# Half-tile score units and one-head masked maxima in a four-block attention kernel

## The chip, the cores and the metric

The kernel runs on one core of one Trainium2 chip. A time is the device time of one execution in microseconds. "Before" was run three times; its median is 3425.52 us (3421.22 to 3428.02).

The core's engines work side by side, each with its own queue: TensorE (PE), whose weight loads the profile shows apart (PEld), VectorE (DVE), ScalarE (ACT), GpSimd (POOL) and SyncE (SP), which starts the transfers. They meet at semaphores: each engine counts its finished work, and others wait for a count.

## The reference

Batch 4, sequence 512, width 256, a context of 1601 rows. Four blocks are applied one after the other, each gated and added to `x`:

```
x = x + tanh(g_xattn[0]) * xattn0(layernorm(x), ctx)            # block 1: 16 heads of 64, no mask
x = x + tanh(g_ffn[0])   * ffn0(layernorm(x))                   # block 2: 16 heads of 16 over 512, then a
                                                                #   top-2 mixture of 8 experts with capacity
x = x + tanh(g_xattn[1]) * xattn1(ctx, ctx, layernorm(x), mask) # block 3: 16 heads of 16 over 1601, masked
x = x + tanh(g_ffn[1])   * ffn1(layernorm(x))                   # block 4: 16 heads of 16 over 512 + 8 experts
```

All attentions are softmax attentions. Block 3 is the one that matters most here:

```
energy = einsum('nqhd,nkhd->nhqk', q, k)
energy = where(mask == 0, -1e20, energy)
attn = softmax(energy / sqrt(256), axis=3)
out = einsum('nhql,nlhd->nqhd', attn, v)
```

## The kernel before

**Slim attentions.** Blocks 2, 3 and 4 have heads of 16. Four heads make a group (`GROUPS` = 4 for each batch). A head's queries and keys lie in 32 partitions, so TensorE's array is used as 32x32 positions: a head stands on its own 32 rows of the array. A matmul of fp32 numbers shows as two records in the trace.

For each batch `b` and group `g` there are these units of work:
- `low`: queries for the maxima, in bf16.
- `max3` (block 3) or `maxb` (blocks 2 and 4): score products in bf16, of which only each query's maximum is kept. Block 3 has 32 `max3` for a group: 4 query tiles, 4 chunks of 401 context columns (`CTX_CHUNKS`), 2 pairs of heads. One unit is eight matmuls (two heads, four column groups) into one slot, and on VectorE two `tensor_tensor_reduce` of 401 columns which add the mask's row and take the maximum. Their thrown-away output goes to one of three places in turn (`max_junk`, in `rest` and `slim`).
- `negb`, `strip`, `rowb`: the maxima, negated and turned, are added to the fp32 queries. After `rowb` a group's scores may begin.
- `scoreb`: for 128 keys and all four heads, the score products in fp32. In block 3 a bf16 product of the mask comes first, into the same accumulation. A group has 13 such tiles in block 3 and 4 in blocks 2 and 4. ScalarE takes the exponential.
- `pvb`: the values times the exponentials of one tile, summed in the PSUM tile `pv`; it uses all rows of the array.
- `tailb`: the division by the sum, at a group's end. `outb` is the projection after four groups, `projqk`, `v4` and `expert4` are block 4's projections and expert products, which use the whole array.

**The ring.** PSUM holds `ring`, three slots of two banks, and `pv`. A unit that needs a slot waits until the engine that last read this slot has finished. A `max3` takes one slot, until VectorE has both its maxima. A `scoreb` takes two: heads 0 and 1 in the first, heads 2 and 3 in the second. Its matmuls for the first pair are sent after the first slot's wait; then PE waits for the second slot (`second_free`) and sends the rest. Nothing can stand between the two.

**The order.** `build_order` puts the units in one sequence, in which every engine takes its own part. Two streams of digits, `TURNS_1` up to the last `ranks` of block 2 and `TURNS_3` behind the experts, say which of eight generators gives the next unit (in `TURNS_3`: 1 block 3's scores, 2 its values, 3 its maxima, 5 to 7 block 4). `Pace` is a small planner which gives each unit a time on each engine. It decides which slot a unit takes (the one that it thinks free first) and where spare matmuls (`warm`) go in, which keep PE at work. It treats TensorE as one thing that is busy or not.

**The first group.** The first 32 `max3` of block 3 have no scores to go with. Three spare matmuls stand behind each.

## Time and profile before

| | us |
|---|---|
| median of three runs | 3425.52 |
| lowest, highest | 3421.22, 3428.02 |
| the profiled execution | 3398.36 |
| its span, first to last instruction | 3396.6 |
| PE busy in the span | 3242.2 |
| DVE, ACT, POOL busy | 1980.8, 1446.3, 955.0 |

The profile is of one execution. Its sections give the busy time of each engine, what released each wait, and the chain of work that ended last. The end of a matmul is modelled, and PE counts as busy when any part of its array is. "idle before" in brackets is time in which that engine did nothing ahead of the row; the arrow names the instruction that ended it. For PE the wait stands at the weight load (PEld), since the loads are sent first.

### The profile page before, as it was taken

Reading aid. Unit: us, or ns where it says so; the run is one execution under the profiler, and the core shown is the slowest. Engines: PE = TensorE matmul, PEld = TensorE weight load, DVE = VectorE, ACT = ScalarE, POOL = GpSimd, SP = SyncE. Lnnn points to the kernel's source line nnn. Section 1 sums busy time; section 2 is a strip of 40 time slices with the busy share of each in tenths; the row PEclk is TensorE's granted clock in tenths of the full one; section 3 lists DMA queues with packets and bytes.
Section 4 is the critical chain, followed back from the end, with each engine's and each line's share of the span. In section 5 each row is a group of like instructions: output and inputs, shape, how many; then the busy total and the mean of one; then the engine's idle time right before and its main releaser. Section 6 shows DMA issues by size and latency. Waiting matters only on the chain.

```text
span 3396.6 us, 71446 instructions
## 1 busy us (share of the span) xinstructions
PE 3242.2 (95%) x30986; PEld 1431.6 (42%) x31007; DVE 1980.8 (58%) x4289; ACT 1446.3 (43%) x1645; POOL 955.0 (28%) x469
## 2 busy tenths in 40 slices
PE   7999999999999999999997979899999999999999
PEld 3444444444434444444433753223333334343344
DVE  4444456554655546565575028677777777766446
ACT  3444344445434453344433212355454454545533
POOL 4655554654465445555400000100000000000000
PEclk9999999999999999999988999899999999999989
DMA  4000000000000000000021622565343444443300
GB/s 152 12 13 13 28 12 15 7 11 33 7 21 12 13 28 7 21 12 12 4 116 39 188 81 75 132 175 158 97 120 115 127 124 117 118 118 113 115 26 20
DMA packets 85306, 221.17 MB, mean 65 GB/s; under 512 B 18424, under 2 KB 39168, under 8 KB 84224
## 3 DMA queue, kind: packets, MB, share of 16 engines
q1 hardware_dynamic: 79616, 201.65, 19.5%
q0 software_dynamic: 5376, 14.95, 2.0%
q8 instruction: 244, 4.00, 0.5%
q14 instruction: 70, 0.57, 0.1%
HBM read 204.61 MB, written 18.48 MB: 66 GB/s over the span
## 4 chain that ended last, share of the span: by engine, by line
PE 84%; DVE 6%; ACT 4%; POOL 3%; issue 1%; DMA 1%; ACTq 0%; POOLq 0%; DVEq 0%
PE ring L1294 13%; PE pv L1179 10%; PE ring L1168 9%; PE pv L1310 9%; PE ring L1246 3%; PE ring L1149 3%; PE ring L1140 3%; PE ring L1126 3%; PE ring L1141 3%; PE ring L1165 3%; PE ring L1127 2%; PE ring L1290 2%; POOL wide L1554 2%; PE ring L1367 2%; PE ring L1348 2%; PE ring L1260 2%
## 5 line engine op out<-in xcount | busy, mean ns | idle before, releaser
L1554 POOL TENSOR_TENSOR wide<-wide 124x1024 f32<-124x1024 f32 (+1 forms) x341 | 803.9, 2358 | 180.2 <-ACT wide L1450 142.2
L1457 ACT ACTIVATE wide<-ring 128x1024 f32<-128x1024 f32 (+1 forms) x544 | 536.2, 1023 | 498.4 <-PE ring L1294 494.6
L1671 DVE TENSOR_REDUCE max_a<-ring 128x2 f32<-128x802 f32 x512 | 493.4, 991 | 395.9 <-PE ring L1149 395.5
L1450 ACT ACTIVATE wide<-ring 124x1024 f32<-124x1024 f32 (+1 forms) x416 | 425.3, 1026 | 438.1 <-PE ring L1168 385.0
L1294 PE MATMUL ring<-slim 32*32 32x512 f32 (+1 forms) x7040 | 522.9, 607 | 0.3 <-DVE slim L1724 0.2
L1699 DVE CUSTOM_DVE_ANT_0 rest<-ring,slim 128x401 bf16<-128x401 f32 x683 | 374.9, 576 | 106.0 <-PE ring L1246 71.1
L1168 PE MATMUL ring<-wide 64*124 64x512 f32 (+1 forms) x1664 | 424.7, 588 | 0.0
L1179 PE MATMUL pv<-wide 124*64 124x512 f32 (+1 forms) x1664 | 413.9, 613 | 8.2 <-ACT wide L1450 8.2
L1709 DVE TENSOR_REDUCE slim<-ring 128x2 f32<-128x1024 f32 x256 | 308.0, 1222 | 111.9 <-PE ring L1260 105.4
L1524 POOL DMA_DIRECT2D slim<-in_ctx_k x16 | 8.9, 558 | 968.5 <-PE ring L1246 920.2
L1551 POOL TENSOR_TENSOR wide<-wide 124x1024 f32<-124x1024 f32 x31 | 73.1, 2357 | 599.5 <-ACT wide L1450 586.2
L1699 DVE CUSTOM_DVE_ANT_0 slim<-ring,slim 128x401 bf16<-128x401 f32 x341 | 195.8, 574 | 59.1 <-PE ring L1246 46.8
L1310 PE MATMUL pv<-wide,slim 128*17 128x512 f32 (+1 forms) x1664 | 226.4, 617 | 0.0
L1294 PEld LDWEIGHTS ring<-slim 32*32 32x32 f32 (+2 forms) x7040 | 173.3, 110 | 114.6 <-issue 73.8
L1246 PE MATMUL ring<-slim 32*32 32x401 bf16 x4096 | 192.0, 347 | 21.4 <-ACT wide L1457 8.8
L1179 PEld LDWEIGHTS pv<-wide 124*64 124x64 f32 (+1 forms) x1664 | 99.0, 136 | 229.2 <-issue 201.4
L1168 PEld LDWEIGHTS ring<-wide 64*124 64x124 f32 (+1 forms) x1664 | 155.5, 183 | 73.0 <-issue 50.4
L1246 PEld LDWEIGHTS ring<-slim 32*32 32x32 bf16 x4096 | 59.8, 88 | 288.6 <-ACT wide L1457 152.1
L1165 PE MATMUL ring<-wide,select_b 64*128 64x512 bf16 x832 | 159.0, 379 | 8.1 <-ACT wide L1450 6.1
L1149 PE MATMUL ring<-wide 64*128 64x401 bf16 x1024 | 155.5, 337 | 9.7 <-DVE max_a L1671 4.7
L1290 PE MATMUL ring<-slim,ident_b 32*32 32x512 bf16 (+1 forms) x3264 | 154.0, 394 | 10.9 <-ACT wide L1457 8.2
L1140 PE MATMUL ring<-wide 128*124 128x128 f32 (+1 forms) x832 | 162.1, 276 | 0.4 <-DVE max_a L1671 0.4
(238 smaller groups left out, 3964.3 us busy)
## 6 DMA issues: line engine op xcount, KB each, us to landing
slim<-masks SPq DMA_DIRECT2D x832, 128.0 KB, 2.7
slim<-in_ctx_k SPq DMA_DIRECT2D x16, 800.5 KB, 4.6
wide<-in_w_pair SPq DMA_DIRECT2D x32, 384.0 KB, 3.0
wide<-in_w SPq DMA_DIRECT2D x16, 512.0 KB, 4.7
wide<-in_we SPq DMA_DIRECT2D x16, 512.0 KB, 3.7
slim<-in_ctx_v SPq DMA_DIRECT2D x16, 442.0 KB, 5.9
wide<-in_ctxT SPq DMA_DIRECT2D x4, 1601.0 KB, 6.8
slim<-in_ctx_k POOLq DMA_DIRECT2D x16, 400.2 KB, 4.8
```

Source lines behind the costliest of these rows:

```text
L1140: pe.matmul(place, ctxT[:, 0, k0:k0 + kn], pair_weights(p)[:, 2, 0, :], start=True, stop=False)
L1168: last = pe.matmul(slot[0:kn, h * BANK:(h + 1) * BANK], keys_a[own, p % 2, k0:k0 + kn], queries_a[own, p % 2, :], start=False, stop=True)
L1179: last = pe.matmul(pv_a[64 * h:64 * h + 64, :], values_a[0:kn, p % 2, k, 64 * h:64 * h + 64], exps_a[0:kn, slot_of["scorea", b, p, k], h * ...
L1246: last = pe.matmul(slot[j * PAD:(j + 1) * PAD, i * BANK:i * BANK + CHUNK], queries_low(3, g)[own, q * P + j * PAD:q * P + (j + 1) * PAD], ...
L1294: last = pe.matmul(head_bank(unit, h)[c0:c0 + cn, :], key_columns(blk, g, k0)[own, c0:c0 + cn], queries_place(blk, g)[own, :], start=blk ! ...
L1310: last = pe.matmul(pv_of[blk][PAD * h:PAD * h + rows_h, :], value_columns(blk, g, k, kn, h), exps_tile(blk, b, g, k, h)[0:kn, :], start=k ...
L1450: sc.activation(exps_a[0:kn, slot_of[unit], :], slot[0:kn, :], ACT.Exp, scale=WIDE ** -0.5).then_inc(scalar_done, 1)
L1457: sc.activation((exps_2 if blk == 2 else exps_34)[0:kn, first + 2 * i:first + 2 * i + 2, :].rearrange("p h n -> p (h n)"), ring_t[0:kn, ba ...
L1554: po.tensor_tensor(sums[0:kn, :], sums[0:kn, :], view, ALU.add).then_inc(pool_done, 1)
L1671: ve.reduce_max(max_a[:, :, q, c], slot.rearrange("p (h n) -> p h n", h=2)[:, :, 0:CHUNK], AX.X).then_inc(vector_done, 1)
L1699: ve.tensor_tensor_reduce(out=max_junk[junk], in0=slot[:, i * BANK:i * BANK + CHUNK], in1=maskQ_sb[:, q, CTX_CHUNKS[c]:CTX_CHUNKS[c] + CHUNK],
L1709: ve.tensor_reduce(neg_cols[blk][:, q, 2 * hp * PAD:2 * hp * PAD + PAD + 1:PAD], slot.rearrange("p (h n) -> p h n", h=2), AX.X, ALU.max, n ...
```

## The change

1. **Score tiles in halves.** A `scoreb` of blocks 2, 3 and 4 becomes two units, `("scoreb", blk, b, g, k, half)`. Each takes one slot, serves two heads, and has one exponential. They may stand apart in the order. In the order string each has its own digit.
2. **Masked maxima.** A `max3` unit is now one head and two chunks, where it was two heads and one chunk. It is still eight matmuls in one slot, but they use four positions of the array, each twice. VectorE takes both chunks with one `tensor_tensor_reduce` of 802 columns. For this `maskQ` is laid out by chunks of 401 (1604 columns), `max_b` gets two columns where it had four, the three `max_junk` places are twice as long, and some areas of `slim` move by four columns.
3. **The planner.** `Pace` has a busy time for each of the four row groups (`rows=`), and counts units on different rows as running side by side, each finished after its own time; `ISSUE` is the time between two sends. The two-slot parts go.
4. **The order.** `TURNS_1` is the old string with each 6 doubled. `TURNS_3` is new (1363 digits before, 1635 after).

```diff
-            turned = self.pe + (DIVIDE if step.parts[0] != self.parts else 0.0)
-            at = max(at, turned)
...
+            at = max(at, self.issued)
+            if step.parts[0] != self.parts:
+                free = max(self.busy) + DIVIDE
+            else:
+                free = max(self.busy[r] for r in step.rows)
...
+            self.issued = at + ISSUE
+            end = max(at, free) + step.pe
+            for r in range(4):
+                self.busy[r] = end if r in step.rows else max(self.busy[r], end - step.pe) if step.parts[0] != self.parts else self.busy[r]
+            self.pe, self.parts = max(self.busy), step.parts[1]
...
-    "maxb": (1, 0, 1, 0), "max3": (1, 0, 2, 0), "negb": (0, 0, 1, 0), "rowb": (1, 0, 1, 0),
-    "scoreb": (2, 2, 0, 0), "pvb": (1, 0, 0, 0), "tailb": (0, 1, 4, 0),
+    "maxb": (1, 0, 1, 0), "max3": (1, 0, 1, 0), "negb": (0, 0, 1, 0), "rowb": (1, 0, 1, 0),
+    "scoreb": (1, 1, 0, 0), "pvb": (1, 0, 0, 0), "tailb": (0, 1, 4, 0),
...
+            place = expo.take()
+            for half in range(2):
+                unit = ("scoreb", blk, b, g, k, half)
+                yield Step(lasts, (("sc", 1.02),), 1, (("rowb", blk, b, g),) + ((("pvb", blk, *behind),) if behind else ()), unit,
+                           divided, rows=(2 * half, 2 * half + 1))
+                plan.slot[unit], plan.slot_free[unit] = place, expo.free[place]
+                emit(in_slot(unit, "scalar"))
...
-                    b, g, q, hp, c = a
+                    b, g, q, h, c = a
...
+                    own = slice(PAD * h, PAD * (h + 1))
                     for i, j in product(range(2), range(P // PAD)):
-                        own = slice(PAD * (2 * hp + i), PAD * (2 * hp + i + 1))
+                        c0 = CTX_CHUNKS[2 * c + i]
...
-                    for first in (0, 2):
-                        if first:
-                            for lane, other in plan.second_free[unit]:
-                                past.wait_ge(*at(lane, *other))
...
+                    for i, (c0, cn) in product(range(2 if blk == 3 else 0), parts):
+                        own = slice(PAD * (2 * half + i), PAD * (2 * half + i) + cn)
+                        pe.matmul(slot[c0:c0 + cn, i * BANK:(i + 1) * BANK], ident_b[own, own],
+                                  mask_places[n % MASK_PLACES][own, c0 // PAD, :], start=True, stop=False)
...
+                    after(junk_free[0])
+                    ve.tensor_tensor_reduce(out=max_junk[junk].rearrange("p (i n) -> p i n", i=2),
+                                            in0=slot.rearrange("p (i n) -> p i n", i=2)[:, :, 0:CHUNK],
+                                            in1=maskQ_sb[:, q, 2 * c * CHUNK:2 * (c + 1) * CHUNK].rearrange("p (i n) -> p i n", i=2),
+                                            scale=1.0, scalar=-3e38, op0=ALU.add, op1=ALU.max,
+                                            accum_out=max_b[:, h, q, c:c + 1]).then_inc(vector_done, 1)
```

What this does to the order of instructions, at three places. In the fences a row is a line of the file, the operation, its tiles and the size of its output, and how often it follows itself. In before, L1246 is a masked maximum (eight matmuls), L1290 the mask and L1294 the scores of one pair of heads, L1310 a value step, L1260 a maximum of block 4.

PE before, block 3 in the first batch, one tile with four maxima between two value steps:

```order
L1310 MATMUL pv<-wide,slim 17x512 x4
L1246 MATMUL ring<-slim 32x401 x16
L1290 MATMUL ring<-slim,ident_b 32x512 x8
L1294 MATMUL ring<-slim 32x512 x8
L1290 MATMUL ring<-slim,ident_b 32x512 x8
L1294 MATMUL ring<-slim 32x512 x8
L1246 MATMUL ring<-slim 32x401 x16
L1310 MATMUL pv<-wide,slim 17x512 x4
```

PE of the changed kernel, the same batch; its L1244, L1283, L1287 and L1303 are the four of before:

```order
L1303 MATMUL pv<-wide,slim 17x512 x4
L1283 MATMUL ring<-slim,ident_b 32x512 x8
L1287 MATMUL ring<-slim 32x512 x8
L1244 MATMUL ring<-slim 32x401 x16
L1283 MATMUL ring<-slim,ident_b 32x512 x8
L1287 MATMUL ring<-slim 32x512 x8
L1244 MATMUL ring<-slim 32x401 x16
L1303 MATMUL pv<-wide,slim 17x512 x4
```

The two maxima that stood ahead of the tile now stand between its halves.

PE before, the last batch of block 4, behind a projection:

```order
L1294 MATMUL ring<-wide 32x512 x32
L1260 MATMUL ring<-wide 32x512 x8
L1310 MATMUL pv<-wide 17x512 x4
L1260 MATMUL ring<-wide 32x512 x8
L1294 MATMUL ring<-wide 32x512 x16
```

PE of the changed kernel there (L1287 scores, L1258 maximum, L1303 value step, L1098 spare matmuls):

```order
L1287 MATMUL ring<-wide 32x512 x16
L1098 MATMUL pv<-consts,ident_b 128x512 x2
L1258 MATMUL ring<-wide 32x512 x8
L1287 MATMUL ring<-wide 32x512 x8
L1258 MATMUL ring<-wide 32x512 x8
L1303 MATMUL pv<-wide 17x512 x4
```

The second tile's halves stand apart, with a maximum between them.

VectorE before and VectorE of the changed kernel, a group's masked maxima. First before:

```order
L1699 ISA rest,max_b<-ring,slim 128x401
L1699 ISA max_b 128x1
L1699 ISA slim,max_b<-ring,slim 128x401
L1699 ISA max_b 128x1
```

Then the changed kernel:

```order
L1688 ISA slim,max_b<-ring,slim 128x802
L1688 ISA max_b 128x1
```

One reduction of 802 columns stands for two of 401.

## Rows read from the trace of the kernel before

**Rows 1.** The page, summary: busy us (share of span) xinstructions.
```profile
span 3396.6 us, 71446 instructions
PE 3242.2 (95%) x30986; PEld 1431.6 (42%) x31007; DVE 1980.8 (58%) x4289; ACT 1446.3 (43%) x1645; POOL 955.0 (28%) x469
```

**Rows 2.** Stretches: length, busy PE PEld DVE ACT POOL, PEclk, DMA share, GB/s.
```profile
0.00:2010.80 2010.80, 1929.63 (x10499) 927.83 (x10507) 1030.31 (x1461) 821.32 (x972) 916.43 (x422) 0.98 0.11 35
2010.80:2078.60 67.80, 48.06 (x402) 17.92 (x411) 46.97 (x170) 2.43 (x5) 9.25 (x10) 0.87 0.10 28
2078.60:3264.70 1186.10, 1147.45 (x18911) 427.27 (x18912) 822.68 (x2527) 581.38 (x620) 29.37 (x37) 0.97 0.44 123
3264.70:3396.60 131.90, 117.06 (x1178) 58.62 (x1180) 80.88 (x131) 41.13 (x49) 0.00 (x0) 0.92 0.05 17
```

**Rows 3.** Waits of PE's loads, 2078.6 to 3264.7: us, times, longest.
```profile
PEld ring L1246 <- ACT wide L1457: 152.1, 196, 1.7
...
PEld ring L1290 <- DVE max_b L1699: 85.6, 147, 1.7
...
PEld ring L1246 <- DVE max_b L1699: 63.3, 97, 7.8
```

**Rows 4.** The costliest VectorE groups: shapes, count, busy us, mean ns, idle before.
```profile
L1671 DVE TENSOR_REDUCE max_a<-ring 128x2 f32<-128x802 f32 x512 | 493.4, 991 | 395.9 <-PE ring L1149 395.5
L1699 DVE CUSTOM_DVE_ANT_0 rest<-ring,slim 128x401 bf16<-128x401 f32 x683 | 374.9, 576 | 106.0 <-PE ring L1246 71.1 <-PE ring L1294 30.1 <-PE ring L1260 0.2
```

**Rows 5.** Timeline, two tiles of block 3: start us, length us, what, count.
```profile
2225.60 0.31 PEld L1246 LDWEIGHTS ring<-slim 32*32 32x32 bf16 x16 [0.85 <-ACT wide L1457]
...
2226.04 0.58 DVE L1699 CUSTOM_DVE_ANT_0 rest<-ring,slim 128x401 bf16<-128x401 f32 x1
2226.20 1.04 PE L1294 MATMUL ring<-slim 32*32 32x512 f32 x16
...
2226.54 0.57 DVE L1699 CUSTOM_DVE_ANT_0 slim<-ring,slim 128x401 bf16<-128x401 f32 x1
...
2227.17 0.11 PEld L1290 LDWEIGHTS ring<-slim,ident_b 32*32 32x32 bf16 x8 [0.84 <-DVE max_b L1699]
...
2227.40 1.04 PE L1294 MATMUL ring<-slim 32*32 32x512 f32 x16
...
2228.68 0.58 DVE L1699 CUSTOM_DVE_ANT_0 slim<-ring,slim 128x401 bf16<-128x401 f32 x1 [0.57 <-PE ring L1246]
...
2228.80 1.05 PE L1310 MATMUL pv<-wide,slim 128*17 128x512 f32 x8
...
2229.78 0.36 PE L1246 MATMUL ring<-slim 32*32 32x401 bf16 x8
...
2233.62 0.11 PEld L1246 LDWEIGHTS ring<-slim 32*32 32x32 bf16 x8 [0.85 <-ACT wide L1457]
```

**Rows 6.** Timeline, a masked maximum behind a second half.
```profile
2205.87 0.41 PE L1246 MATMUL ring<-slim 32*32 32x401 bf16 x8
...
2206.27 0.62 PE L1294 MATMUL ring<-slim 32*32 32x512 f32 x3
2207.02 0.58 DVE L1699 CUSTOM_DVE_ANT_0 slim<-ring,slim 128x401 bf16<-128x401 f32 x1 [1.77 <-PE ring L1294]
```

**Rows 7.** Timeline, two maxima behind a half, no value step.
```profile
2214.99 2.02 ACT L1457 ACTIVATE wide<-ring 128x1024 f32<-128x1024 f32 x2 [0.60 <-PE ring L1294]
...
2217.05 0.11 PEld L1290 LDWEIGHTS ring<-slim,ident_b 32*32 32x32 bf16 x8 [0.88 <-ACT wide L1457]
...
2218.45 1.02 ACT L1457 ACTIVATE wide<-ring 128x1024 f32<-128x1024 f32 x1 [1.45 <-PE ring L1294]
```

**Rows 8.** Timeline, both halves of a block 4 tile at once.
```profile
3245.79 1.16 PE L1294 MATMUL ring<-wide 32*32 32x512 f32 x32
```

**Rows 9.** Timeline, the first group's maxima, loads of two in a row.
```profile
2050.42 0.11 PEld L1246 LDWEIGHTS ring<-slim 32*32 32x32 bf16 x8 [0.42 <-DVE max_b L1699]
...
2051.46 0.11 PEld L1246 LDWEIGHTS ring<-slim 32*32 32x32 bf16 x8 [0.42 <-DVE max_b L1699]
```

197 lines of the change are left out of this document (83 added, 114 removed).

## The prediction

> I call a unit of slim scores a half-tile: eight 32x32 positions of the array (two heads, four column groups), one slot of the three-slot PSUM ring, one exponential. Two halves make a tile. A masked maximum (`max3`) also takes one slot. In the changed stretch there are 272 tiles (208 of block 3, 64 of block 4), 512 masked maxima and 128 maxima of block 4.
>
> **What bounds the kernel now.** First the page's summary, then the busy time by stage, then who ended each wait, then the timeline at single tiles. The summary shows PE busy for 3242 of 3397 us and no other engine over 58% [rows 1]. The stages [rows 2]: wide attention with block 2 and the experts fill 0 to 2011 us, the hand-over and the first group's maxima 68 us, the mixed stretch of blocks 3 and 4 1186 us, the last batch of block 4 132 us. In the mixed stretch PE counts as busy for 1147 us, but much of that is a part of the array working alone, and the weight loads show where the queue stood: before masked maxima and score tiles it waited 152 us for an exponential and 86 and 63 us for a maximum, each of which had to free a ring slot [rows 3]. So the stretch is bound by PE's own queue, which stops at slots, not by array work.
>
> The timeline shows one tile with four maxima [rows 5]. Two maxima load at 2225.60, the first half follows, and the second half's loads come only at 2227.17, after 0.84 us without a load, when a maximum has freed a slot. Its matmuls start 1.20 us after the first half's (2226.20 and 2227.40), although they stand on other rows of the array. Then two maxima and the value matmuls at 2228.80, and the next tile's maximum loads at 2229.78: 4.18 us. The next tile, with three maxima, begins there and ends at 2233.62: 3.84 us. Where two slots are free, both halves pass in 1.16 us together [rows 8], against 1.04 us of matmuls for one alone in [rows 5]; the stop between the halves costs about 1.1 us in this tile.
>
> **The change, part by part.** The first order string is the old one with each score digit doubled, and units and slots up to the experts stay where they were; the two-slot wait there stood between the halves already. I cost it, the experts and the differently laid out row mask (three columns more) at nothing: a stretch of 2011 us without a moved instruction. What the change can move is the 1386 us behind it.
>
> *Vector work.* Before, a masked maximum is two reductions of 401 columns, 576 ns each; a reduction over 802 columns takes 991 ns [rows 4], so 0.415 us for 401 columns more. In [rows 5] one reduction follows the other after 0.50 us (2226.04, 2226.54), so a unit holds the engine 1.00 us. The new unit needs 0.50 + 0.415 = 0.915 us. That is 512 x 0.08 = 43 us of vector work less. Only what PE waits for counts: about 290 waits for a maximum in the mixed stretch, the largest two groups being 147 and 97 [rows 3]. At 0.08 us each that is 23 us, at 0.15 us, where two follow each other, 43 us. In a tile with four maxima an exponential frees the next slot at nearly the same moment, so part is lost: I take -15 us, bounds -40 and 0.
>
> *Array work of a maximum.* Its eight matmuls now use four positions twice. In [rows 5] eight at once take 0.36 us; the second round adds 401 columns, about half of that, 0.17 us. Behind a score half this is hidden. It shows in some 50 of the 512, where a value step waits right behind: +8 us, bounds 0 and +30.
>
> *The halves apart.* Counted in the two PE orders, between one half and the next there stood nothing 289 times (272 of these within a tile), and now 144 times. New are two maxima alone (3 before, 41 now), two maxima and a value step (9, 88), one maximum alone (0, 66), a maximum and a value step (6, 51). What each costs depends on when the maxima behind a half are reported. In [rows 6] a maximum's matmuls start at 2205.87 and last 0.41 us, while the last three score matmuls, which stand ahead of them in the program, start at 2206.27 and last 0.62. Starts of separate rows of the array do pass each other. VectorE had been idle for 1.77 us when it began at 2207.02, after the scores' end at 2206.89: the maximum was reported after the half, not at its own end near 2206.28. The planner in the new file counts such a maximum as finished after its own 0.36 us, so it is reported some 0.6 us later than planned.
>
> The Trainium skill, "TensorE: Matmul & The Clock Gate", section "Why this matters for your kernels", says that concurrent matmuls complete in exact program order. By that rule the four-maximum tile below takes 4.9 us; by the planner's reading it would be 0.6 us shorter, since a maximum would free the next slot ahead of the exponential. The trace agrees with the rule on completion. The same page (section "Step-by-step: what each phase is for") has matmuls stay in program order altogether; for the starts [rows 6] differ, and the measurement decides.
>
> So the price of two maxima alone between halves is that of the three slots: half, maximum, maximum. The next half waits for the exponential. [rows 7]: exponentials end at 2217.01, the half loads at 2217.05, the next exponential starts at 2218.45; 0.04 + 1.40 + an exponential of 1.02 us is 2.46 us from half to half. A value step of 1.05 us fits inside. A four-maximum tile so written costs 4.92 us, against 4.18 before: 41 x 0.74 = **+30 us**, bounds +10 (if its neighbours make up for it) and +40.
>
> One maximum between halves: the second half needs the third slot, and ends about 1.1 us after the first, as it does now, but a maximum lies hidden in it. That maximum costs before what divides the two tiles of [rows 5], 4.18 - 3.84 = 0.34 us. Half of it is lost to the later report: 66 x 0.17 = **-11 us**, bounds -25 and 0.
>
> The 144 remaining neighbours: they now mostly follow a value step, so two slots have had a microsecond to come free, where before a maximum stood right ahead. The second half costs between 0.12 us [rows 8] and 1.2 us [rows 5], before mostly near the latter; I take a quarter microsecond less for half of them: **-18 us**, bounds -60 and 0.
>
> *The ends.* The first 32 maxima run alone, one in 1.04 us (2050.42 to 2051.46) [rows 9], with three spare matmuls behind each; 0.08 us less of VectorE, 0.17 us more of PE, which is about full there: between -3 and +5, taken +1. In the last batch three groups have maxima between the halves, each of 1.22 us on VectorE: 0 to +6, taken +3. No DMA moves by more than a unit: mask loads still follow the second half, and four places are ahead.
>
> **Sum**: -15 + 8 + 30 - 11 - 18 + 1 + 3 = -2 us. The profiled execution took 3398.4 us (span 3396.6), 27.1 us under the median of the runs shown, 3425.5. So 3396 us in a profile's terms, and **3423 us** in the median's. All low bounds together give -120 us, all high ones +80 us; they don't come together, so the case's own range is 25 us either way, 3398 to 3448.
>
> **The rivals.** *The plan holds* (faster): the halves are freed of the slot wait. Exponentials and maxima end 152 + 86 + 63 = 301 us of waits in [rows 3]. If 15% of these goes, 45 us, the time is 3380. For it speaks that the idle time ahead of second halves is real, and that expert steps now stand between halves in places, under which a slot comes free for nothing. Against it speak [rows 6].
>
> *The late report decides* (slower): 129 pairs of maxima stand right behind a half. If each pair's tile loses 0.74 us as in the sum above for those with a value step too, and only the neighbours' gain comes back, it is 129 x 0.74 / 2 - 18 = +30 us: 3455. VectorE then stands idle while a half ends and gets two maxima at once. [rows 5] already show that wait, 0.57 us before the first maximum behind a second half. The point from which it decides is about 70 such pairs.
>
> *The change does nothing*: if VectorE's shorter work and the order cancel because one chain (scores, exponential, slot) bounds both, the time is that of before, 3425; it lies inside the forecast's case. The granted clock is a price on top: 0.97 in the mixed stretch [rows 2]; a stop in a new place can cost or give 10 us, which widens the range.
>
> **How the numbers follow.** Gains and losses cancel to 25 us either way: 0.50. The plan holds: 0.26. The late report decides: 0.24. The least that a measurement can tell from no change is about 0.2%, 7 us. Inside the first case I split 0.18 faster, 0.16 same, 0.16 slower. Together faster 0.44, same 0.16, slower 0.40. The range takes in most of both rivals: 3365 to 3465.
>
> **What would show it.** The stretch up to the experts' end stays at 2011 us. A masked maximum is one reduction near 0.99 us, VectorE's busy time falls by about 40 us. Tiles written half, two maxima, half, two maxima, value step take 4.9 us (late report) or 4.3 (plan). The waits of [rows 3] for a maximum shrink, those for an exponential stay or grow. A maximum behind a half, with VectorE idle, starts after that half's end. I am wrong if the mixed stretch moves by over 25 us; then it shows in the length of those tiles, or in the waits of groups at rowb, which I left as they are.

## The result and the profile after

The changed kernel takes 3542.39 us (median of 4 runs, 3538.65 to 3544.89), the kernel before 3426.77 us (4 runs, 3421.22 to 3428.10): 1.034 of it, 95% interval 1.0322 to 1.0358. It is 116 us slower. The forecast was 3423 us, with a range that ended at 3465. The profiled execution took 3544.89 us; its span of 3543.1 us stands against 3396.6 us in [rows 1], 146.5 us more. That is more than the change costs, since the profiled execution of before was 27 us under its median. A second profile of the changed kernel (e8 below), beside a kernel before of 3399.64 us, has a span of 3503.7 us, 107 us over [rows 1]; amounts of time are therefore taken from e8. One execution of e13 below (4222 us, granted clock 0.73) was in a slower state and is left out of its median and ratio.

The page of the changed kernel, its summary (busy us, share of the span, instructions):

```profile
span 3543.1 us, 70384 instructions
PE 3336.2 (94%) x31007; PEld 1426.5 (40%) x31007; DVE 1941.8 (55%) x3265; ACT 1458.1 (41%) x1645; POOL 955.2 (27%) x469
```

VectorE has 39 us less to do than in [rows 1], as reckoned. PE shows 94 us more, although no product was added. The stretches of the changed kernel, columns as in [rows 2]:

```profile
0.00:2010.80 2010.80, 1930.23 (x10497) 925.55 (x10498) 1029.87 (x1460) 821.53 (x972) 916.54 (x422) 0.98 0.11 35
...
2010.80:2078.60 67.80, 49.44 (x354) 16.94 (x352) 40.05 (x95) 1.43 (x3) 7.71 (x8) 0.85 0.09 26
...
2078.60:3543.10 1464.50, 1356.48 (x20163) 484.06 (x20158) 871.83 (x1713) 635.13 (x670) 30.99 (x39) 0.91 0.36 101
```

Up to 2010.8 us nothing moved. All of the loss lies behind. The same last stretch of the kernel before, whose two parts stand in [rows 2], in one line:

```profile
2078.60:3396.60 1318.00, 1264.51 (x20086) 485.88 (x20090) 903.56 (x2658) 622.51 (x669) 29.37 (x37) 0.96 0.40 113
```

1464.5 against 1318.0 us: the whole 146.5. The granted clock is 0.91 where it was 0.96. In these two traces it has two levels, 1.0 and 0.5 (2.4 and 1.2 GHz), so a mean of 0.96 over 1318 us is about 105 us at the lower level, and 0.91 over 1464.5 us about 264 us. Added up record by record it is 101 and 256 us, and 192 us in e8.

The waits of PE's loads in the changed kernel, 2078.6 to 3419 us (us in total, times, longest), which answer [rows 3]. L1283 is the mask product with which a half begins, L1244 a masked maximum, L1303 a value step:

```profile
PEld ring L1283 <- DVE max_b L1688: 175.9, 148, 2.8
PEld pv L1303 <- issue: 157.6, 262, 1.7
PEld ring L1244 <- DVE max_b L1688: 94.7, 133, 2.4
...
PEld ring L1283 <- ACT wide L1448: 47.4, 55, 2.1
PEld ring L1244 <- ACT wide L1448: 38.3, 50, 2.4
```

A half waited 85.6 us for a maximum in [rows 3]; now it is 175.9 us (164.8 in e8), in the same number of waits (147 and 148): each is twice as long. A maximum waited mostly for an exponential (152.1 us), now mostly for another maximum. The waits of PE moved from ScalarE to VectorE, though VectorE has less to do.

The masked maxima among the costliest VectorE groups, to be held against [rows 4]:

```profile
L1688 DVE CUSTOM_DVE_ANT_0 slim<-ring,slim 128x802 bf16<-128x802 f32 x341 | 333.4, 992 | 193.2 <-PE ring L1287 113.4
...
L1688 DVE CUSTOM_DVE_ANT_0 rest<-ring,slim 128x802 bf16<-128x802 f32 x171 | 169.6, 992 | 90.0 <-PE ring L1287 61.6
```

992 ns, as estimated. And one turn of the new order's most frequent pattern (half, two maxima, value step) in the timeline of the changed kernel, at the full clock, as [rows 5] has the old one:

```profile
2584.37 1.05 PE L1303 MATMUL pv<-wide 128*17 128x512 f32 x8
...
2584.40 1.02 ACT L1448 ACTIVATE wide<-ring 128x1024 f32<-128x1024 f32 x1 [1.46 <-PE ring L1287]
2584.50 0.99 DVE L1688 CUSTOM_DVE_ANT_0 slim<-ring,slim 128x802 bf16<-128x802 f32 x1 [0.63 <-PE ring L1244]
...
2585.42 0.99 DVE L1688 CUSTOM_DVE_ANT_0 slim<-ring,slim 128x802 bf16<-128x802 f32 x1
2585.55 0.11 PEld L1283 LDWEIGHTS ring<-slim,ident_b 32*32 32x32 bf16 x8 [1.05 <-DVE max_b L1688]
...
2585.65 0.35 PE L1244 MATMUL ring<-slim 32*32 32x401 bf16 x4
...
2586.47 0.12 PEld L1244 LDWEIGHTS ring<-slim 32*32 32x32 bf16 x8 [0.56 <-DVE max_b L1688]
...
2586.92 1.05 PE L1303 MATMUL pv<-wide 128*17 128x512 f32 x8
2586.95 1.02 ACT L1448 ACTIVATE wide<-ring 128x1024 f32<-128x1024 f32 x1 [1.52 <-PE ring L1287]
```

From value step to value step 2.55 us, in which one half and two maxima pass. ScalarE works 1.02 us of it and waits 1.52 for PE, VectorE waits 0.63 for PE, PE waits 1.05 and 0.56 for VectorE. Nobody is full; the three pass three slots around. Two such turns are a tile with four maxima: 5.1 us.

### The profile page after: what moved, and what is told of

Same layout as the page of the kernel before. It is cut to its first block, busy times and chain, and to the rows that moved or that the text cites. A ratio compares the mean times of both kernels' runs of the same rounds, so it can differ in the third digit from the quotient of the medians.

```text
span 3543.1 us, 70384 instructions
## 1 busy us (share of the span) xinstructions
PE 3336.2 (94%) x31007; PEld 1426.5 (40%) x31007; DVE 1941.8 (55%) x3265; ACT 1458.1 (41%) x1645; POOL 955.2 (27%) x469
## 4 chain that ended last, share of the span: by engine, by line
PE 82%; DVE 7%; issue 4%; ACT 3%; POOL 3%; DMA 1%; DVEq 0%; SPq 0%; POOLq 0%; ACTq 0%
PE ring L1287 14%; PE pv L1176 10%; PE ring L1165 9%; PE pv L1303 8%; PE ring L1283 3%; PE ring L1244 3%; PE ring L1146 3%; PE ring L1137 3%; PE ring L1123 3%; PE ring L1138 3%; PE ring L1162 2%; PE ring L1124 2%; POOL wide L1544 2%; PE ring L1360 2%; PE ring L1341 2%
## 5 line engine op out<-in xcount | busy, mean ns | idle before, releaser
L1448 ACT ACTIVATE wide<-ring 128x1024 f32<-128x1024 f32 (+1 forms) x544 | 548.4, 1024 | 617.5 <-PE ring L1287 569.0
L1287 PE MATMUL ring<-slim 32*32 32x512 f32 (+1 forms) x7040 | 579.2, 642 | 1.5 <-issue 1.0
L1688 DVE CUSTOM_DVE_ANT_0 slim<-ring,slim 128x802 bf16<-128x802 f32 x341 | 333.4, 992 | 193.2 <-PE ring L1287 113.4
L1244 PE MATMUL ring<-slim 32*32 32x401 bf16 x4096 | 266.8, 363 | 10.9 <-DVE max_b L1688 3.9
L1303 PE MATMUL pv<-wide,slim 128*17 128x512 f32 (+1 forms) x1664 | 260.3, 689 | 3.8 <-ACT wide L1448 3.4
L1283 PE MATMUL ring<-slim,ident_b 32*32 32x512 bf16 (+1 forms) x3264 | 169.9, 413 | 62.6 <-DVE max_b L1688 46.8
L1688 DVE CUSTOM_DVE_ANT_0 rest<-ring,slim 128x802 bf16<-128x802 f32 x171 | 169.6, 992 | 90.0 <-PE ring L1287 61.6
L1287 PEld LDWEIGHTS ring<-slim 32*32 32x32 f32 (+1 forms) x7040 | 171.0, 114 | 115.9 <-issue 80.6
L1283 PEld LDWEIGHTS ring<-slim,ident_b 32*32 32x32 bf16 (+1 forms) x3264 | 48.7, 88 | 299.3 <-DVE max_b L1688 175.9
```

The lines of the kernel that those rows point to most:

```text
L1244: last = pe.matmul(slot[j * PAD:(j + 1) * PAD, i * BANK:i * BANK + CHUNK], queries_low(3, g)[own, q * P + j * PAD:q * P + (j + 1) * PAD], ...
L1283: pe.matmul(slot[c0:c0 + cn, i * BANK:(i + 1) * BANK], ident_b[own, own], mask_places[n % MASK_PLACES][own, c0 // PAD, :], start=True, sto ...
L1287: last = pe.matmul(slot[c0:c0 + cn, i * BANK:(i + 1) * BANK], key_columns(blk, g, k0)[own, c0:c0 + cn], queries_place(blk, g)[own, :], sta ...
L1303: last = pe.matmul(pv_of[blk][PAD * h:PAD * h + rows_h, :], value_columns(blk, g, k, kn, h), exps_tile(blk, b, g, k, h)[0:kn, :], start=k ...
L1448: sc.activation((exps_2 if blk == 2 else exps_34)[0:kn, first:first + 2, :].rearrange("p h n -> p (h n)"), slot[0:kn, :], ACT.Exp, scale=D ...
L1688: ve.tensor_tensor_reduce(out=max_junk[junk].rearrange("p (i n) -> p i n", i=2), in0=slot.rearrange("p (i n) -> p i n", i=2)[:, :, 0:CHUNK ...
```

## The experiments

Eighteen kernels were run, in five groups, each group beside the kernel before on one chip. That one took 3398.5 to 3428.3 us in them, so ratios to it are compared, not times. "Low clock" is the time at the lower level behind 2078.6 us, added up from the clock records of the one profiled execution. Last lines of stretches are shown once, here, in the columns of [rows 2]; all run from 2078.6 us to the kernel's end. In this order: e8 (the changed kernel again), e1, e3, e4, e7, e9, e15, e16:

```profile
2078.60:3503.70 1425.10, 1318.15 (x20149) 479.52 (x20155) 871.36 (x1711) 634.74 (x670) 30.93 (x39) 0.93 0.37 104
```
```profile
2078.60:3430.20 1351.60, 1302.14 (x20118) 500.69 (x20122) 870.67 (x1705) 623.02 (x670) 30.72 (x39) 0.96 0.39 110
```
```profile
2078.60:3506.10 1427.50, 1324.70 (x20090) 481.11 (x20095) 903.49 (x2658) 634.01 (x670) 30.31 (x38) 0.93 0.36 104
```
```profile
2078.60:3467.00 1388.40, 1270.10 (x20095) 470.71 (x20100) 866.49 (x1701) 634.53 (x670) 30.94 (x39) 0.95 0.38 107
```
```profile
2078.60:3390.90 1312.30, 1259.55 (x20093) 485.73 (x20096) 866.01 (x1699) 622.84 (x670) 30.32 (x38) 0.96 0.41 113
```
```profile
2078.60:3493.90 1415.30, 1320.41 (x20084) 473.43 (x20089) 905.16 (x2657) 629.32 (x668) 28.38 (x36) 0.93 0.37 105
```
```profile
2078.60:3520.80 1442.20, 1359.09 (x20116) 495.59 (x20121) 912.14 (x2671) 630.76 (x670) 30.80 (x39) 0.92 0.36 103
```
```profile
2078.60:3585.10 1506.50, 1377.74 (x20120) 495.72 (x20124) 897.69 (x2673) 624.96 (x670) 30.71 (x39) 0.90 0.34 99
```

The results in one table; the texts follow below.

| kernel | order of the last half | maxima | ratio to before | 95% interval | low clock, us |
|---|---|---|---|---|---|
| before | old | old | 1 | | 101 |
| e7 | old | one reduction, two strips | 0.9945 | 0.9925 to 0.9964 | 98 |
| e1 | old | new | 1.0126 | 1.0089 to 1.0163 | 119 |
| e4 | new | one reduction, two strips | 1.0212 | 1.0180 to 1.0245 | 133 |
| e6 | new, slots in turn | new | 1.0293 | 1.0268 to 1.0318 | 209 |
| e8 (after) | new | new | 1.0320 | 1.0288 to 1.0352 | 192 |
| e3 | new | old | 1.0335 | 1.0288 to 1.0382 | 211 |
| e10 | new | new, each issued twice | 1.0527 | 1.0495 to 1.0560 | 182 |

### Order or maxima: e1, e3, e8

The first theory: the new order costs the time. The rival: the maxima do, which now stand on one strip of the array.

e1, the last half's order of before in the changed kernel (first line of the table; 1 and 5 are the score streams of blocks 3 and 4, 3 the stream with the masked maxima, 2 and 6 the value steps):

```diff
 TURNS_3 = (
-    "00333333333333333333333333333333333333333131113213313321331332313133213313321331332133133231323133113233331132"
+    "00333333333333333333333333333333333333333331133311332311303231133233201111323323111120113233231133323113332331"
...
```

> The changed kernel with the last half's order of before (the old table, with a digit that stood for a score tile written twice, since a tile is now two steps). The maxima are the new ones: one head, two chunks, one reduction. If the new order is what costs the 116 us, this is near before, 3415 to 3440 us. If the one-head maxima cost it (344 in the slim part, on one row strip each, 0.36 us of one position where it was 0.17), it stays near after, above 3480 us. If both do a share, it lies between.

e3, the old maxima in the changed kernel:

```diff
-                for c in range(len(CTX_CHUNKS) // 2):
-                    for h in range(GROUP):
+                for c in range(len(CTX_CHUNKS)):
+                    for hp in range(2):
...
+                    for i in range(2):
+                        after(junk_free[0])
+                        ve.tensor_tensor_reduce(out=max_junk[junk][:, 0:CHUNK], in0=slot[:, i * BANK:i * BANK + CHUNK],
+                                                in1=maskQ_sb[:, q, c * CHUNK:(c + 1) * CHUNK],
...
```

> The changed kernel, its order and its planner, with the maxima of before: two heads and one chunk, two reductions of 401 columns. If the new order costs the time, this is as slow as after or slower, 3530 to 3580 us, since VectorE has 0.13 us more for each maximum. If the one-head form of the maxima costs it, this is near before, 3420 to 3450 us.

> The changed kernel, unchanged, beside the others on one chip: ratio to before 1.032 to 1.036, as recorded. It is the yardstick for the kernels of this call.

Measured: 1.0126, 1.0335, 1.0320. (Some expectations count 344 masked maxima. The file has 512, of which 32 belong to the first group.) The order alone, with the old maxima, costs all of it (e3). With the new maxima it costs 1.9% (e8 against e1). But the new maxima alone, in the old order, cost 1.3% (e1), where a gain of 15 us was reckoned. Both theories are half right, and the parts don't add up: 3.35 and 1.26 would be 4.6, the two together give 3.2.

### One strip and one reduction: e4, e7

The new maximum differs in two things: one reduction instead of two, and eight matmuls on four positions instead of eight. e4 takes them apart:

```diff
-                    own = slice(PAD * h, PAD * (h + 1))
                     for i, j in product(range(2), range(P // PAD)):
+                        own = slice(PAD * (h ^ i), PAD * (h ^ i) + PAD)
                         c0 = CTX_CHUNKS[2 * c + i]
```

> The changed kernel, where each maximum's second chunk is taken with the neighbouring head's rows (its maxima are mixed over two heads, so the shifts are others): eight matmuls on eight positions, as before, instead of two rounds on four, and everything else unchanged. If what costs is that a one-head maximum runs its two chunks one after the other on one strip, the time falls by up to 344 x 0.19 = 65 us, to 3475 to 3500 us. If the order or the slots cost it, it stays within 10 us of 3542.

> The changed kernel with the order of before (as the first experiment) and, as in the fourth one, each maximum's second chunk taken with the neighbouring head's rows, so that eight matmuls stand on eight positions (the maxima are mixed over two heads; the shifts are others). Against the first experiment (ratio 1.013 to before) only the array positions change, against before only the single reduction. If one strip costs the same in any order, about 1.3%, this is at or under before: ratio 0.995 to 1.002. If one strip costs only through the slots of the new order, it stays at 1.010 to 1.015.

Measured 1.0212 and 0.9945. So the one strip costs 1.8% in the old order (e1 against e7, some 61 us) and 1.1% in the new one (e8 against e4, 37 us). The single reduction gives 0.55% in the old order (e7 against before, 19 us) and 1.2% in the new one (e4 against e3). The new order costs 2.7% (e4 against e7) with everything else alike. Two cautions: e7 also has the new file's planner and slots, and e3's planner picks other slots than that of e4, so the single reduction isn't quite alone in either pair.

Where the strip is felt shows in the value steps' waits, which need all rows of the array. The waits of value steps' loads, 2078.6 to 3419 us, in e1 and in e7:

```profile
PEld pv L1303 <- issue: 112.4, 273, 0.8
```
```profile
PEld pv L1303 <- issue: 96.0, 273, 1.6
```

A value step behind a one-strip maximum waits 0.34 us in the timelines, behind a two-strip one 0.18 (e4). The two lines differ by 16 us. PE's busy time tells more: 1302.1 us in e1, 1259.6 in e7. The rest is spread thinly: from the end of one score half to the end of the next, with three maxima and a value step between them, it is 2.87 us in e1 and 2.77 in e7 (68 times, means at full clock). That it is the products on the maximum's own rows which wait is argued, not shown. In the new order the low clock differs more, 192 us in e8 and 133 in e4.

### Slots in turn: e6

```diff
-        self.picked = sorted(range(RING), key=lambda i: self.ring[i])[:step.slots]
+        if self.turned:
+            self.picked = [self.turn % RING][:step.slots]
+            self.turn += len(self.picked)
```

> The changed kernel in its own order, but in the last half the three score slots are taken strictly in turn. The new planner, which reckons maxima as done beside the half in front of them, gives 235 units of the last half the slot of the unit two before them (79 in the kernel before), although the matmuls are seen to complete in order. If waiting for such slots costs the time, this is 30 to 80 us faster than after, 3460 to 3510 us. If the order itself costs it, it stays within 10 us of 3542.

Measured 1.0293, on the same chip as e1, e3 and e4; e8 has 1.0320. At most 0.3%, and the intervals overlap. The planner's choice of slots isn't what costs.

### The halves apart: e9, e11, e12, e13, e14

e9 leaves the old order and the old maxima, and moves one step of the maxima's stream between the halves wherever one stood right behind them (113 becomes 131):

```diff
-    "00333333333333333333333333333333333333333331133311332311303231133233201111323323111120113233231133323113332331"
+    "00333333333333333333333333333333333333333331313313132313103231313233201113123323111120131233231313323131332331"
...
```

> The old order and the old maxima (two heads, two reductions), with one edit: in 152 places of the last half a step of the maxima's stream that stood behind the second half of a tile now stands between its halves; in 135 of them it is a maximum. In the trace of before two halves side by side are reported 0.50 us apart in the mean; with one maximum between them they are 1.8 us apart in the changed kernel. If it is the parting of the halves that costs, it is about 135 x 0.4 = 54 us, ratio 1.010 to 1.025. If only two maxima in a row behind a half cost (the price of the forecast), one between is free or a gain: 0.990 to 1.003.

Measured 1.0295: 97 us for 135 maxima, 0.72 us each. The forecast had the opposite sign for it (-0.17 us each). From the end of a first half to the end of its second half, by the records of their last matmuls, it is 0.89 us in the mean in the kernel before (272 tiles), 1.31 us in e9 (1.83 for its 135 parted ones) and 2.64 us in the changed kernel (e8). The 0.50 us in the expectation is too low. The blocks differ: in block 3 of the kernel before it is 1.10 us in the mean and 1.08 in the median (208 tiles), in block 4 0.23 and 0.10 (64 tiles).

The 1.08 us of block 3 is no wait for a slot. In 76 of the 208 tiles the second half's mask products start within 0.5 us of the first's, so both slots were free, and the halves still end 1.08 us apart. The kernel before has such a tile at 2249.56 us; this one is the changed kernel's, behind a value step and at full clock:

```profile
2315.74 0.52 PE L1283 MATMUL ring<-slim,ident_b 32*32 32x512 bf16 x16
...
2315.96 2.12 PE L1287 MATMUL ring<-slim 32*32 32x512 f32 x32
```

The score products of both halves take 2.12 us together, twice the 1.04 of one, while the same 32 records take 1.16 us in block 4 ([rows 8]). Why block 3's halves don't overlap is open. So 1.08 us is there with or without a wait, and a maximum between the halves comes on top of most of it: 1.70 us at full clock for the parted tiles of e9 (105 of them) against 1.05. The timeline of e9:

```profile
2545.76 0.41 PE L1282 MATMUL ring<-slim,ident_b 32*32 32x512 bf16 x8
...
2546.41 0.12 PEld L1243 LDWEIGHTS ring<-slim 32*32 32x32 bf16 x8 [0.30 <-DVE max_b L1688]
...
2547.30 0.11 PEld L1282 LDWEIGHTS ring<-slim,ident_b 32*32 32x32 bf16 x8 [0.77 <-DVE max_b L1688]
```

The second half's mask products start 1.54 us behind the first's, and waited for the slot of a maximum. A third of the 97 us is clock (below): e9 has 191 us of low clock.

The reverse, then: the changed kernel with every pair of halves side by side again, what stood between them behind (e11) or half ahead and half behind (e12); e13 and e14 are the same orders with the old maxima. The first line of e11:

```diff
-    "00333333333333333333333333333333333333333131113213313321331332313133213313321331332133133231323133113233331132"
+    "00333333333333333333333333333333333333333113113211333321133332311333211333321133332113333231132333113233331132"
...
```

> The changed kernel with its own order, but the two halves of every tile are put side by side again: in 174 tiles of the last half what stood between them (maxima, value steps, experts) now stands behind the second half. Everything else keeps its place, and the maxima are the new ones. If the parting of the halves is what the new order costs (0.72 us for each of 135 in the experiment before), most of the difference to the old order goes: ratio to before 1.010 to 1.020, where after is 1.032 and the old order with these maxima 1.013. If the rest of the order (which tile gets which maxima, experts and value steps) costs it, the ratio stays over 1.025. The runs of maxima are longer than in either order (four and a value step 16 times), which may cost some of it.

> As the one before, but half of what stood between the halves is put ahead of the first half and half behind the second, so that maxima are spread more evenly. Ratio to before 1.005 to 1.020 if the parting costs; over 1.025 if not.

> The order of the kernel with the halves side by side and the rest behind, with the maxima of before (two heads, two reductions). If parting and the one-strip maxima together hold the whole loss, this is near before: ratio 0.995 to 1.010. If the order costs otherwise, it stays over 1.015.

> The order with the halves side by side and the rest spread on both sides, with the maxima of before. Ratio 0.990 to 1.010 if parting and one-strip maxima hold the whole loss; over 1.015 otherwise.

Measured 1.0352, 1.0577, 1.0263 and 1.0534 (intervals of 0.2 points either way), low clock in e11 155 us, in e12 342. All four came out where the expectations put them if the rest of the order costs it, and far from the gain that parting alone would have meant. Parting the halves of the old order costs 3%; joining those of the new one gives back 0.7 points with the old maxima (e13 against e3) and nothing with the new ones (e11 against e8). What a parted tile costs depends on where its maxima would stand otherwise.

The traces have a price for that, much the same in both kernels of the table. The time from the end of a half to the end of the next, by what stands between them (block 4's maxima counted in; number of places, and mean at full clock in us):

| between two halves | before | changed (e8) |
|---|---|---|
| nothing | 289: 0.85 | 144: 0.92 |
| one maximum | none | 66: 1.37 |
| a value step | 11: 2.10 | 24: 2.16 |
| one maximum, a value step | 10: 2.27 | 57: 2.17 |
| two maxima | 3: 2.32 | 41: 2.53 |
| two maxima, a value step | 55: 2.59 | 111: 2.54 |
| three maxima, a value step | 68: 2.81 | 22: 2.66 |

A value step beside two maxima costs nothing more in e8, and a third maximum 0.1 to 0.2 us. In e16 below, four maxima and a value step take 3.60 us (82 places). What costs is to open such a place at all. Before has 254 places with something in them, the changed kernel 399. An estimate from the mean prices of all the kernels at full clock puts the new order 50 to 60 us above the old one. The same sum gives 40 us at most for e15 and e17, so it doesn't explain these two.

### How many maxima in a tile: e15 to e18

In the kernel before, tiles with one value step and 0, 1, 2 or 3 maxima (block 4's counted in) last 2.7, 3.8, 3.2 and 4.1 us, from one second half to the next; those with four and two value steps 5.6. (The expectation of e15 has 3.5 us for the first and 5.9 for the last.) Of its 272 tiles, 73 have two and 94 three. The new order has 74 tiles with four and 56 with none: it puts a group's maxima early, four to a tile, and leaves bare tiles at the end. So the third theory was: the price bends upwards, and the new order pays for being uneven. e16 crams the old order in this way, e15 makes it more even; e17 and e18 make the new order even.

```diff
-    "00333333333333333333333333333333333333333331133311332311303231133233201111323323111120113233231133323113332331"
+    "00333333333333333333333333333333333333333113333113323311330233113323320113333113323321133331133233011221121121"
...
```

> The maxima and the order of before, halves side by side, with each group's maxima put as early as they go, four to a tile, and none in the group's last tiles, as the new order has them: tiles with 0, 1, 2, 3 and 4 maxima are 87, 32, 17, 6 and 129. By the prices of before this costs some 110 us: ratio 1.025 to 1.040, like after, with none of the halves parted and none of the maxima changed. If unevenness is not what costs, it stays under 1.010.

> The maxima and the order of before, halves side by side, with the maxima of each group spread more evenly over its tiles: tiles with 0, 1, 2, 3, 4 and over 4 maxima are 32, 18, 93, 116, 12 and 1, where before has 50, 18, 73, 94, 29 and 8. Price of a tile by its maxima, in the trace of before: 0: 2.3 us, 3.5 with a value step; 1: 3.7; 2: 3.4; 3: 4.15; 4: 5.9; 5: 6.7. By these prices it saves some 40 us: ratio to before 0.985 to 0.995. If the number of maxima in a tile does not matter, only their sum, it stays within 0.3% of before, or is slower for whatever else the moves upset.

> The changed kernel's own order and maxima with the halves side by side, as in the eleventh kernel (ratio 1.035), and the maxima of each group spread evenly: tiles with 0, 1, 2, 3 and 4 or more maxima are 28, 28, 86, 117 and 13. If unevenness is what the order costs, this comes down to what the one-strip maxima cost in the old order: 1.005 to 1.018. If not, it stays over 1.025.

> The changed kernel's own order and maxima, with the value steps, experts and fourth block's steps that part halves left where they are (99 tiles stay parted), and only the masked maxima spread evenly, none of them between halves in block 3: tiles with 0, 1, 2, 3 and 4 or more maxima are 32, 15, 110, 94 and 21. If unevenness costs the most and a value step between halves little, 1.010 to 1.025; if parting costs by itself whatever stands between, over 1.025.

Measured: e16 1.0472, e15 1.0263, e17 1.0396, e18 1.0809. Cramming costs what was expected and more, with no half parted and no maximum changed. But the even orders lose as well, and e18, where value steps part 99 tiles, is the slowest of all. So the number in a tile is not the law either. In e15 one piece can be named. About from the first group's row step to the second's, e15 and then the kernel before:

```profile
2082.80:2171.90 89.10, 76.83 (x929) 19.31 (x929) 43.95 (x157) 28.52 (x29) 7.21 (x8) 0.59 0.32 88
```
```profile
2079.50:2137.60 58.10, 52.46 (x935) 16.25 (x939) 43.07 (x157) 27.12 (x28) 6.54 (x8) 0.88 0.51 134
```

The same units (929 and 935 matmuls recorded) in 89.1 us at a clock of 0.59, and in 58.1 us at 0.88. A third of e15's loss of 93 us is this one group.

### Maxima beside experts: e19, e20

e15 had also moved maxima away from expert steps, which keep PE for 3.5 us and need neither ScalarE nor, until their end, VectorE. e20 does this alone for 16 maxima, e19 moves 13 the other way.

```diff
-    "23113233421155323411336411424371132331133231143231136355323311323336437355243341137113446355324113635532337113"
+    "23113233421155323411336411424711332331133231143231136355323311323336437355243341137113446355324113635532711333"
...
```

> The maxima and the order of before, halves side by side, with 13 masked maxima moved ahead, from behind the next tile to right behind an expert step (3.5 us of matmuls for which ScalarE has nothing to do, so a slot and VectorE are free there). If a maximum beside an expert step is free and one in a tile costs some 0.75 us, this is 5 to 10 us faster than before: ratio 0.997 to 0.9985. If its place makes no difference, within 0.1% of before.

> The reverse: 16 masked maxima that stand beside an expert step in before moved behind the next tile. If the cover of the expert steps is what the evened order gave away (it had moved maxima out of there too), this is 12 to 20 us slower than before: ratio 1.0035 to 1.006. If the evened order lost by something else, it stays within 0.15% of before.

Measured: e20 1.0047 (1.0033 to 1.0062), as expected; e19 1.0032 (1.0015 to 1.0049), a miss: it was to be faster. Both moves cost. A caution: e9 and e13 to e16, e19 and e20 use the new file's planner. With the old order and the old maxima it lets 20 of the last half's 1328 slot uses follow on another unit than in the kernel before. That combination was not run, so an offset of a few tenths of a per cent common to e19 and e20 can't be excluded. Against the 2.6 to 4.7% of the others it doesn't matter.

### The clock: e10, and a reading of all traces

> The changed kernel, where each masked maximum's eight matmuls are issued twice (the same values to the same place), 16 in all, so the array is busier between slots and a maximum 0.35 us longer. In the changed kernel the clock stands at its lower level for 256 us of the last half (101 before), with PE 68% busy in the 4 us ahead of most of these spells. If the low clock costs much, the added work keeps it up and pays for a part of itself: at most 20 us slower or even faster than after, and under 150 us of low clock. If the length of the maxima is what costs, it is 50 to 150 us slower than after (344 x 0.35 = 120 us).

```diff
-                    for i, j in product(range(2), range(P // PAD)):
+                    for _, i, j in product(range(2), range(2), range(P // PAD)):
```

Measured 1.0527, 71 us over e8, low clock 182 us against 192. More array work did little for the clock, and it cost a good part of its own length (512 x 0.35 = 179 us at most). What brings the clock down is not settled. Just ahead of its falls PE is shown busy 69% of the time in the changed kernel (median of 44 spells), 68% in the kernel before (14 spells), but 88% in e10 (25 spells).

What a spell costs can be read, since kernels with one order have it in different groups. The last half was cut at the 16 row steps of block 3 and the two last projections. For before, e1 and e7, and for e3, e4, e6 and e8, the length of each piece was set against its low-clock time, with a mean of its own for every piece and every kernel. The slope is 0.37 +- 0.04 us and 0.39 +- 0.03 us for each us of low clock (standard errors). The repeated executions of one kernel on one chip say the same: over 148 executions of 23 such sets, the time grows by 0.39 +- 0.01 us for each us of low clock, the latter reckoned from each execution's mean clock and span. By this, the 91 us more of low clock in e8 are some 35 of its 107 us, e9's 90 us are 35 of its 97, and of the 37 us between e8 and e4 the clock makes 23. Set beside the kernel before on its own chip, e15 has 97 us more of low clock and e18 353: 38 of 93 us and 138 of 276. The rest of these losses isn't clock.

## Why the prediction was wrong, point by point

What failed above all is the price of the order (the part "The halves apart"): forecast at +1 us, it is 91 us. The single terms:

**The first 2011 us unchanged**: right. PE is busy for 1930.2 us there, against 1929.6 in [rows 2].

**Vector work, -15 us (-40 to 0)**: right. The reduction takes 992 ns, VectorE's busy time fell by 39 us, and the single reduction gives 15 to 19 us in the old order (e7; by the slope above some 8 of it come with the clock), 40 in the new.

**Array work of a maximum, +8 us (0 to +30)**: right in kind, mis-sized. It is 61 us in the old order (e1 against e7) and 37 in the new. The step that failed is "behind a score half this is hidden": the value steps wait longer, places with maxima take 0.1 us more, and in the new order there are 59 us more of low clock.

**Two maxima between halves, 41 x 0.74 = +30 us**: the turn was right, the count was not. A turn takes 2.55 us (2.46 forecast), and with a value step in it it is the same: in e8, at full clock, two maxima between halves take 2.53 us in the mean (28 times) and two maxima and a value step 2.54 (72 times). The text itself said that "a value step of 1.05 us fits inside", and then priced only the 41 pairs without one. All 129 at 0.74 us are 95 us. The 0.74 rests on one tile of 4.18 us; against the four maxima together of e16 (3.60 + 1.08 = 4.68 us) two turns cost 0.4 us more, and 129 of them some 50 us. The rival "the late report decides" had them, but halved the sum without a row to show for it, and came to +30.

**One maximum between halves, 66 x -0.17 = -11 us**: wrong sign. e9 has +0.72 us each, about 0.5 without the clock. The base was right: the second half ends about 1.1 us after the first in block 3. The step that failed is that it "ends about 1.1 us after the first, as it does now, but a maximum lies hidden in it". With a maximum between them the halves are 1.70 us apart in e9 at full clock. In the changed kernel such a place takes 1.37 us, 0.5 more than one with nothing in it (0.85); and a maximum taken out of a place with three saves about 0.2 us, not 0.34.

**The remaining neighbours, -18 us (-60 to 0)**: there is no sign of it. In block 3 at full clock they end 1.07 us apart in e8 (93 places) and 1.04 in the kernel before (212). The failed step is the lower bound, 0.12 us by [rows 8]: that row is of block 4. In block 3 the second half ends 1.08 us after the first even with both slots free, so two free slots give nothing back, and the "stop between the halves" of [rows 5] was mostly no stop.

**The clock, 10 us either way**: mis-sized, about 35 us (e8).

**Completion in order**: nothing here speaks against it. The late report of [rows 6] is seen again in the turn shown above (VectorE idle 0.63 us before the first of two maxima). So the new planner reckons short. By its own sums the last half takes 1272 us in the new order and 1344 in the old; made to complete in order it has 1323 for the new one. Of the 72 us that it saw to gain, 51 vanish so. It still prefers the order that the chip runs slower, so this is not its only error: it has no clock, and it runs block 3's halves side by side.

The planner also says something on the experiments that could have been known ahead. By its sums the last half takes 1405 us in e9, 1377, 1412, 1404 and 1452 in e13 to e16, and 1374, 1400, 1402 and 1433 in e11, e12, e17 and e18, against 1344 in the old order. It has the sign right for every order that was moved by hand, but reckons the loss 30 to 190 us smaller than it is against before. Only the order that comes with the change, which it rates best, does it rate wrongly. So the slowness of the moved orders is weak evidence on why the new one is slow.

In sum: of the 3.2% of e8, the order makes 2.7, the one strip 1.1, and the single reduction gives 0.55 back (they are e7, e4 and e8 in turn: -0.55, +2.67, +1.08; taken in another turn the order is 1.9 or 3.35, so these are shares along one path). The order's 30 - 11 - 18 = +1 us stand against 91 us (2.67%). Two gains that don't exist, -11 and -18, cancelled a loss that was counted for a third of its places; that the strip's 8 us were 37 comes on top. The chance of 0.40 for "slower" was spread over sums that ended at +40 us.

What stays open: which property of an order decides. Parting halves (e9), cramming (e16), evening (e15, e17, e18) and joining (e11 to e14) of the two orders all lose against before, by 2.6 to 8%, and low clock goes along (e18: 471 us, e16: 310). The prices of places explain about half of the new order's loss and the clock about a third; why evened orders have more low clock, and what the rest of their loss is, none of the three theories says.

A version that beats both with each head's own maxima was not found. e7 is faster than before by 0.55%, but it mixes two heads' maxima; the same layout with the right values needs a second copy of the low queries and keys in the neighbouring strips, with a product or a copy more for each of 16 groups. That wasn't tried.

## What to carry to other kernels

Price a changed order by the mean of a kind of gap over the whole trace, not by one tile, and price every gap of the same kind; and take the row for a bound from the same block, since two halves pass in 1.16 us in block 4 and in 2.12 in block 3. A planner that orders work on concurrent rows must report in program order, or it sees a gain that isn't there (51 of 72 us here). And a unit made cheaper on one engine (one reduction instead of two) isn't cheaper if it stands twice as long on the array that all wait for: swap one part at a time. Here only the single reduction paid, in e7.

## What the runs showed of the hardware

- Two halves on separate rows of the array, side by side in the queue, end 0.10 us apart in block 4 (median of 64) and 1.08 us apart in block 3 (median of 208), there also when both slots are free; with a maximum between them 1.72 us (median of 135, e9).
- The clock falls without a long stop. In the changed kernel PE's loads wait 2.8 us at most for a slot of a maximum in the mixed stretch, and it still has 256 us of low clock, in 44 spells.
- A us at the lower clock costs 0.37 to 0.39 us here; but one group can stay there for most of its length (89.1 us at a clock of 0.59 in e15).
- An order with the same work can be 6.7% slower (e18 against e1, 8.1% against before), with PE shown busy for 92% of the stretch (1493.8 of 1620.9 us), hardly less than before (96%):

```profile
2078.60:3699.50 1620.90, 1493.79 (x20170) 518.34 (x20178) 874.61 (x1715) 635.61 (x670) 31.54 (x39) 0.85 0.32 92
```
